# Cross attention of an eight-batch transformer step: k, q, x and masks prepared two batches ahead, rows of maxima sent from GpSimd, set-up woven into the first runs

## The chip, the cores and the metric

One core of a Trainium2 chip runs the whole program in one launch. The metric is the device time of that launch in microseconds; lower is better. A core has five engines with an instruction stream each (TensorE, VectorE, ScalarE, GpSimd, SyncE, in rows PE, DVE, ACT, POOL, SP) that work side by side and wait for each other by semaphores, and 16 DMA engines that move data for whoever issues a transfer.

## The reference

x is (8, 512, 256) in float32, with a context of the same shape. Four residual layers follow each other; in each, ln() is a layer norm without weights:

```python
x = x + feature_attention(ln(x), ctx, ctx)          # softmax over the sequence, per feature
x = x + experts(ln(x))                              # 8 experts, top 2
# the layer that the change touches: 16 heads of 16
q, k, v = heads(ln(x) @ Wq.T + bq), heads(ctx @ Wk.T + bk), heads(ctx @ Wv.T + bv)
scores = where(mask == 0, -1e9, q @ k.T / 4)
x = x + merge(softmax(scores) @ v) @ Wo.T + bo
x = x + gated_self_attention(ln(x))                 # 8 heads of 64, top 3 gates
```

The mask holds ones alone in these inputs. The program tests that at run time (a flag) and runs a loop without mask products when nothing is masked; the one thing that it then still takes from the mask is rv, which says for each query whether any key is left.

## The kernel before, in words

The layers are blocks of their own, one after the other; each block ends when all five engines have. The change lies in the block `cross_attention`. Before it, `combine` loads the weights and the context of batch 0. After it come `self_gates` and `self_attention`.

**Units and runs.** The 16 heads are four groups of 4. A unit is one group of one batch: 32 units, four for each batch, in a loop over batches (`pe.Fori(0, B)`, written once for each engine). A unit has 16 slots (4 heads by 4 blocks of 128 keys or queries) in 8 runs of two. In each slot TensorE makes two score products of 64x512: `score_b` (L915), the scores of this unit with keys on partitions, which ScalarE exponentiates (L1020), and `score_a` (L901), the scores of the unit two later with queries on partitions, of which VectorE takes the maximum of each row (L1108). The maxima must be known before the exponentials: they enter `score_b` as two extra rows of the stacked q. In even runs TensorE also multiplies the exponentials by the values (`values`, L921).

**Stacks.** q and k are split into a head and a rest part (float32 from two reduced parts). The parts of all heads go to DRAM (`store`, 1 MB for q, 1 MB for k) and come back group by group as stacks of 3 x 16 rows of each half, by `load_stack(g)`: 14 DMAs a group, issued by SP when the exponentials of unit g are done. `score_a` of group 0 of batch b+1 is in unit 2 of batch b, that of group 1 in unit 3, of groups 2 and 3 in units 0 and 1 of the next iteration.

**Jobs.** All other TensorE work shares one PSUM bank, `misc`, and so goes in a fixed order, one job a run at most, written out in `JOBS` as (name, unit, run), each after the score products and values of its run:
- m: transposes the maxima of the next unit (L837). ScalarE copies them, GpSimd splits them in two rows (`split_rows`), and SP sends them into the stack by four DMAs (`send_rows`).
- k0, k1, q0, q1, v0, v1: halves of the projections of the next batch; xT0, xT1: transposes of its normed x; rv: from the transposed mask. For q GpSimd makes the parts (`split_q`), for v it spreads the values (`move_values`).
- n0 to n3: transposes of a unit's output, divided by the sums on VectorE; t0, t1, o0, o1: the output projection of the batch before.

TensorE, in order, waits before a job until `misc` is free, and for v and k until the context is in (`ctx_in`). What an engine's stream has behind a waiting instruction waits too.

**Set-up.** `FIRST` lists the jobs for batch 0, which run one after the other. Then come the stacks, 16 runs of `score_a` alone (two units), the rows of maxima of unit 0, and the loop.

**SP's stream in an iteration**: masks of the next batch; rows for unit 1; store k (after k1); rows for unit 2; store q (after q1); stack 0, 1; rows for unit 3; stack 2; context of batch b+2; rows for the next unit 0; stack 3. Everything that SP issues goes in one queue.

Of the kernel before, what the change touches and what calls it, by code (L numbers as in the profile page):

```python
# [5 lines left out]
ALU = mybir.AluOpType  # L6
# [673 lines left out]
def cross_attention(nc, io, x, mv, rstd, ident, ones, bias, flag, q_parts, k_parts, weights, ctxT, w_in, ctx_in):  # L680
# [10 lines left out]
    with ExitStack() as ctx:  # L691
# [3 lines left out]
        ident16, tiny16 = m.sb("ident16", [P, P], BF16), m.sb("tiny16", [P, P], BF16)  # L695
        xn, xT = m.sb("xn", [P, TB, D]), m.sb("xT", [P, KC, S])
        nb, nbT = m.sb("nb", [P, 2, TB, S], BF16), m.sb("nbT", [P, 2, TB, S], BF16)
# [4 lines left out]
        k_stack = [m.sb(f"k_stack{g}", [P, HG // 2, S], F32R) for g in range(G)]  # L702
        negmax = m.sb("negmax", [P, 2, 2, 2, TB])
# [13 lines left out]
        nb_in, nbT_in = m.sem("nb_in"), m.sem("nbT_in")  # L717
# [19 lines left out]
        JOBS = [("m", 0, 0), ("k0", 0, 1), ("n0", 0, 2), ("k1", 0, 3), ("xT0", 0, 4), ("xT1", 0, 5), ("rv", 0, 6), ("q0", 0, 7),  # L737
# [3 lines left out]
        LAST = ["n0", "t0", "t1", "o0", "o1"]  # L741
        FIRST = ["k0", "k1", "xT0", "xT1", "rv", "q0", "q1", "v0", "v1", "m"]
# [10 lines left out]
        def nxt(b):  # L753
            return b + 1 if isinstance(b, int) else (b + 1) % B
# [1113 lines left out]
```

## Time and profile before

| | us |
|---|---|
| median of 3 runs | 2672.16 |
| lowest, highest | 2660.42, 2674.15 |
| the profiled execution | 2665.32 |
| its span, first to last instruction | 2663.6 |
| PE busy in the span | 2122.1 (80%) |
| DVE busy | 1484.3 (56%) |
| ACT busy | 926.3 (35%) |
| POOL busy | 836.8 (31%) |
| the cross loop, first score to last exponential | 1074.2 to 1677.5 |

The profile is one execution, with a start and a length for each instruction. Its views: busy time of each engine in chosen stretches, with the granted clock of TensorE (1 is 2.4 GHz, 0.5 is 1.2 GHz) and what the DMA engines moved; waits, put down to what ended them; instructions in order of time; and DMAs with the time from issue to landing. "L901" is line 901 of the kernel. A released wait stands in brackets behind the instruction that had waited.

### The profile page before, as it was taken

How to read it: one execution, taken by the hardware profiler on the slowest of the kernel's cores; microseconds unless marked ns; L12 is line 12 of the kernel's file. 1: busy time of each engine (PE TensorE's matmuls, PEld its weight loads, DVE VectorE, ACT ScalarE, POOL GpSimd, SP SyncE). 2: the span in 40 equal slices, each digit the busy share in tenths (PEclk: the TensorE clock that was granted, in tenths of full speed). 3: DMA queues.
4: the chain of work that ended last, by engine and by line, in shares of the span. 5: the costliest groups of instructions: out<-in, count | busy, mean ns of one | idle time of the engine just before them, and what ended most of it. 6: DMA issues, size and time to landing. Idle time of an engine off the chain costs nothing. (4 is left out here: it accounts for less than half of the span.)

```text
span 2663.6 us, 37640 instructions
## 1 busy us (share of the span) xinstructions
PE 2122.1 (80%) x11952; PEld 1389.3 (52%) x11961; DVE 1484.3 (56%) x2297; ACT 926.3 (35%) x1539; POOL 836.8 (31%) x753
## 2 busy tenths in 40 slices
PE   2340899999999505889888888838999999999997
PEld 1340899999999502333333333614545545554554
DVE  7820454545554344567666666544656656656655
ACT  2410333333333200455555555312333333333332
POOL 0067553435550362122212222011323323333232
PEclk9999999999999856899999999669999999999999
DMA  3162332333322332232232232324233223223322
GB/s 126 63 243 101 111 115 79 117 122 110 122 78 65 109 88 88 89 102 89 82 104 84 87 98 86 118 53 95 58 73 86 65 68 86 69 61 86 76 56 64
DMA packets 149071, 244.68 MB, mean 92 GB/s; under 512 B 22502, under 2 KB 71310, under 8 KB 146698
## 3 DMA queue, kind: packets, MB, share of 16 engines
q1 hardware_dynamic: 109762, 164.07, 21.9%
q0 software_dynamic: 11104, 44.06, 4.8%
q10 hardware_dynamic: 28160, 35.99, 4.2%
q8 instruction: 25, 0.41, 0.1%
q14 instruction: 20, 0.16, 0.0%
HBM read 120.48 MB, written 67.04 MB: 70 GB/s over the span
## 5 line engine op out<-in xcount | busy, mean ns | idle before, releaser
L1108 DVE TENSOR_REDUCE ca_negmax<-ca_na 128x2 f32<-128x1024 f32 x272 | 332.4, 1224 | 153.6 <-PE ca_na L901 153.6
L1020 ACT ACTIVATE ca_pr<-ca_st 128x512 f32<-128x512 f32 x512 | 278.9, 597 | 206.6 <-PE ca_st L915 205.6
L901 PE MATMUL ca_na<-ca_k_stack,ca_q_stack 64*128 64x512 f32 x544 | 222.7, 489 | 59.0 <-DMA ca_q_stack<-ca_zrow 55.6
L592 DVE TENSOR_TENSOR ex_h<-ex_up,ex_sg 128x512 f32<-128x512 f32 x136 | 94.1, 692 | 306.8 <-ACT ex_sg L555 197.4
L1706 DVE TENSOR_REDUCE sa_negmax<-sa_na 128x1 f32<-128x512 f32 x272 | 182.7, 674 | 130.8 <-PE sa_na L1527 126.5
L915 PE MATMUL ca_st<-ca_q_stack,ca_k_stack 64*128 64x512 f32 x512 | 210.6, 473 | 29.5 <-ACT ca_pr L1020 26.5
L515 PE MATMUL ex_gp<-ex_xp,moe_gu_p 128*128 128x256 f32 x1632 | 221.8, 286 | 1.4 <-DVE ex_xp L578 1.4
L515 PE MATMUL ex_up<-ex_xp,moe_gu_p 128*128 128x256 f32 x1632 | 218.4, 284 | 0.0
L528 PE MATMUL ex_yp<-moe_dn_p,ex_hp 128*128 128x256 f32 x1632 | 208.8, 286 | 11.3 <-DVE ex_hp L582 11.3
L515 PEld LDWEIGHTS ex_gp<-ex_xp,moe_gu_p 128*128 128x128 f32 x1632 | 206.1, 193 | 2.4 <-DVE ex_xp L578 1.8
L528 PEld LDWEIGHTS ex_yp<-moe_dn_p,ex_hp 128*128 128x128 f32 x1632 | 198.8, 192 | 15.2 <-DVE ex_hp L582 15.2
L515 PEld LDWEIGHTS ex_up<-ex_xp,moe_gu_p 128*128 128x128 f32 x1632 | 206.2, 193 | 0.0
L1694 POOL TENSOR_TENSOR sa_acc<-sa_acc,sa_pr 128x1024 f32<-128x1024 f32 x64 | 151.4, 2366 | 170.3 <-ACT sa_pr L1645 170.3
L1690 POOL TENSOR_TENSOR sa_acc<-sa_pr 128x1024 f32<-128x1024 f32 x32 | 75.1, 2348 | 386.5 <-ACT sa_pr L1645 386.5
L253 POOL TENSOR_TENSOR moe_gu_p<-moe_gu_raw,all_ones 128x512 fp32r<-128x512 f32 x64 | 85.9, 1377 | 287.0 <-PE ex_mark L532 263.8
L1645 ACT ACTIVATE sa_pr<-sa_st 128x1024 f32<-128x1024 f32 x128 | 131.1, 1024 | 107.5 <-PE sa_st L1536 107.5
L915 PEld LDWEIGHTS ca_st<-ca_q_stack,ca_k_stack 64*128 64x128 f32 x512 | 83.6, 191 | 152.3 <-ACT ca_pr L1020 98.7
L921 PE MATMUL ca_av<-ca_pr,ca_vw 128*32 128x512 f32 x1056 | 148.0, 635 | 0.0
L1535 PE MATMUL sa_st<-sa_q,sa_k 128*128 128x512 f32 x256 | 146.2, 571 | 0.0
L1543 PE MATMUL sa_av<-sa_pr,sa_vw 128*64 128x512 f32 x528 | 141.8, 617 | 0.0
L582 DVE TENSOR_TENSOR ex_hp<-ex_h,ex_hp 128x512 fp32r<-128x512 f32 x136 | 130.1, 960 | 2.0
L874 PE MATMUL ca_misc<-cross_ctxT,cross_wk 128*128 128x512 f32 x72 | 38.1, 655 | 113.3 <-DVE ca_zrow L1149 106.8
(261 smaller groups left out, 3798.1 us busy)
## 6 DMA issues: line engine op xcount, KB each, us to landing
sa_q<-sa_qh SPq DMA_DIRECT2D x140, 128.0 KB
sa_k<-sa_kh SPq DMA_DIRECT2D x140, 128.0 KB
ex_raw_m<-masks ACTq DMA_DIRECT2D x34, 512.0 KB, 3.8
moe_gu_raw<-gateupT POOLq DMA_DIRECT2D x8, 2048.0 KB, 8.2
ca_q_stack<-q_parts SPq DMA_DIRECT2D x216, 64.0 KB
ca_k_stack<-k_parts SPq DMA_DIRECT2D x216, 64.0 KB
expert_rows<-rt_zeros SPq DMA_DIRECT2D x20, 512.0 KB, 15.9
k_parts<-ca_kp SPq DMA_DIRECT2D x9, 1024.0 KB, 4.3
```

Source lines behind the costliest of these rows:

```text
L515: last = pe.matmul(out[:, f, :], gu_p[e % 2][:, wr, c, col:col + P], xp[:, xr, c, :], start=(n == 0), stop=(n == 3 * KC - 1))
L528: last = pe.matmul(yp[:, i, :], hp[:, hr, f, i * P:(i + 1) * P], dn_p[e % 2][:, wr, f, :], start=(n == 0), stop=(n == 3 * FC - 1))
L901: last = pe.matmul(na[r % 2][:, i, :], q_stack[g][rows, i, t * P:(t + 1) * P], k_stack[g][rows, i, :], start=not masked, stop=True)
L915: pe.matmul(st[i][:, :], k_stack[g][rows, i, t * P:(t + 1) * P], q_stack[g][rows, i, :], start=not masked, stop=True).then_inc(st_full, 1)
L921: last = pe.matmul(av[32 * h:32 * h + 32, :], vw[:, g, t, h, :], pr[:, t % 2, h % 2 * 2 + h // 2, :], start=(t == 0), stop=(t == TB - 1), ...
L1020: act.activation(pr[:, s // HG % 2, s % HG, :], st[s % 2][:, :], ACT.Exp, scale=DK ** -0.5).then_inc(exp_done, 1)
L1108: dve.tensor_reduce(negmax[:, g % 2, 1 - r % 2, :, r // 2], na[r % 2][:, :, :], AX.X, ALU.max, negate=True).then_inc(max_done, 1)
L1535: pe.matmul(out, k1[c][:, h, t * P:(t + 1) * P], q1[c][:, h, :], start=True, stop=False)
L1543: last = pe.matmul(av[h * H:(h + 1) * H, :], vw[:, c, t, h * H:(h + 1) * H], pr[:, t, h, :], start=(t == 0), stop=(t == TB - 1), skip_grou ...
L1645: act.activation(pr[:, t, :, :], st[t % 2][:, :, :], ACT.Exp, scale=H ** -0.5).then_inc(exp_done, 1)
L1694: pool.tensor_tensor(acc[:, :, :], acc[:, :, :], pr[:, t, :, :], ALU.add).then_inc(acc_done, 1)
L1706: dve.tensor_reduce(negmax[:, par, h, t:t + 1], na[s % 2][:, :], AX.X, ALU.max, negate=True).then_inc(max_done, 1)
```

## The change

- k, q, xT and rv are prepared for batch b+2 in iteration b, in place of b+1; v still for b+1. `JOBS` deals the same 21 jobs to other runs: the tail of the batch before (t, o) comes first, then v and rv, then k, then q.
- k reads a context buffer of its own, `ctxK`, loaded two batches ahead; v still reads `ctxT`. The transposed masks get a third buffer.
- SP's iteration: masks, transposed masks, context for v (b+1), context for k (b+2); the four stacks, each when its unit's exponentials are done; then a wait for all four, the store of k and the store of q. The first four stand at the head of the loop, where they follow the stores of the iteration before.
- The rows of maxima are sent by GpSimd, in `split_rows`, right behind the split; `send_rows` is gone from SP.
- Set-up: `FIRST` holds jobs for batch 0 and batch 1; those of batch 1 and the first m stand at places 2 to 13 among the 16 runs of `score_a` (None: before them, as till now). The two last iterations prepare batches that nobody uses.
- In ScalarE's stream the jobs of run 0 come ahead of the copy of the unit's output; VectorE norms x after run 0, not run 1; GpSimd spreads one group of values a unit and splits q in unit 3.

```diff
+        ctxK = m.sb("ctxK", [P, KC, S])
...
-        nb, nbT = m.sb("nb", [P, 2, TB, S], BF16), m.sb("nbT", [P, 2, TB, S], BF16)
+        nb, nbT = m.sb("nb", [P, 2, TB, S], BF16), m.sb("nbT", [P, 3, TB, S], BF16)
...
-        nb_in, nbT_in = m.sem("nb_in"), m.sem("nbT_in")
+        nb_in, nbT_in, ck_in = m.sem("nb_in"), m.sem("nbT_in"), m.sem("ck_in")
...
-        JOBS = [("m", 0, 0), ("k0", 0, 1), ("n0", 0, 2), ("k1", 0, 3), ("xT0", 0, 4), ("xT1", 0, 5), ("rv", 0, 6), ("q0", 0, 7),
-                ("m", 1, 0), ("q1", 1, 1), ("t0", 1, 2), ("t1", 1, 3), ("n1", 1, 4),
-                ("m", 2, 0), ("v0", 2, 1), ("n2", 2, 2), ("v1", 2, 5),
-                ("m", 3, 0), ("n3", 3, 2), ("o0", 3, 3), ("o1", 3, 7)]
+        JOBS = [("m", 0, 0), ("n0", 0, 3), ("xT0", 0, 4), ("t0", 0, 5), ("xT1", 0, 6), ("t1", 0, 7),
+                ("m", 1, 0), ("v0", 1, 1), ("n1", 1, 2), ("o0", 1, 3), ("v1", 1, 5), ("rv", 1, 7),
+                ("m", 2, 0), ("k0", 2, 1), ("n2", 2, 2), ("o1", 2, 3), ("k1", 2, 5),
+                ("m", 3, 0), ("q0", 3, 1), ("n3", 3, 3), ("q1", 3, 5)]
         LAST = ["n0", "t0", "t1", "o0", "o1"]
-        FIRST = ["k0", "k1", "xT0", "xT1", "rv", "q0", "q1", "v0", "v1", "m"]
+        FIRST = [("k0", 0, None), ("k1", 0, None), ("xT0", 0, None), ("xT1", 0, None), ("rv", 0, None), ("q0", 0, None), ("q1", 0, None),
+                 ("v0", 0, None), ("v1", 0, None), ("xT0", 1, 2), ("xT1", 1, 3), ("rv", 1, 5), ("k0", 1, 6), ("m", 0, 7),
+                 ("k1", 1, 9), ("q0", 1, 11), ("q1", 1, 13)]
...
+        def batch(name, b):
+            return b + 1 if name[0] == "v" else b + 2
...
-            def send_rows(g, a):
-                sp.wait_ge(ml_ready, a + 1)
-                for r in range(2):
-                    for j in range(2):
-                        row = j * HALF + RM + r
-                        sp.dma_start(q_stack[g][row:row + 1, :, :].bitcast(F32).rearrange("a i (t n) -> a (i t) n", n=P),
-                                     mrow[j * 2 * TB:(j + 1) * 2 * TB, r, :].bitcast(F32)).then_inc(m_in, 16)
+            load_context(sp, io, ctxK, ck_in, 1)
+            load_bias_T(0, 0)
+            load_bias_T(1, 1)
             load_bias(0, 0)
             sp.wait_ge(set_up, SETUP)
-            store(kp, k_parts, misc_free, k_stored, FIRST.index("k1") + 1)
+            store(kp, k_parts, misc_free, k_stored, first("k1", 0) + 1)
             store(qp, q_parts, qp_ready, q_stored, KC)
             sp.wait_ge(k_stored, 16)
             sp.wait_ge(q_stored, 16)
             for g in range(G):
                 load_stack(g)
-            sp.wait_ge(misc_full, FIRST.index("v1") + 1)
-            load_context(sp, io, ctxT, ctx_in, 1)
-            send_rows(0, 0)
+            for g in range(G):
+                sp.wait_ge(stack_in[g], LOAD)
+            store(kp, k_parts, misc_free, k_stored, first("k1", 1) + 1)
+            store(qp, q_parts, qp_ready, q_stored, 2 * KC)
             with sp.Fori(0, B) as b:
                 sp.wait_ge(exp_done, b * G * SLOTS + 2)
-                for g in range(G):
-                    sp.wait_ge(stack_in[g], b * LOAD + LOAD)
-                load_bias(nxt(b), (b + 1) % 2)
-                send_rows(1, b * G + 1)
-                store(kp, k_parts, misc_free, k_stored, b * nj + (nf + number("k1") + 1))
-                send_rows(2, b * G + 2)
-                store(qp, q_parts, qp_ready, q_stored, b * KC + 2 * KC)
+                load_bias((b + 1) % B, (b + 1) % 2)
+                load_bias_T((b + 2) % B, (b + 2) % 3)
+                load_context(sp, io, ctxT, ctx_in, (b + 1) % B)
+                load_context(sp, io, ctxK, ck_in, (b + 2) % B)
                 for g in range(G):
                     sp.wait_ge(exp_done, b * G * SLOTS + ((g + 1) * SLOTS + 2))
...
                    if g == 0:
                         sp.wait_ge(k_stored, b * 16 + 32)
                         sp.wait_ge(q_stored, b * 16 + 32)
                     load_stack(g)
-                    if g == 1:
-                        send_rows(3, b * G + 3)
-                    if g == 2:
-                        load_context(sp, io, ctxT, ctx_in, (b + 2) % B)
-                        send_rows(0, b * G + 4)
-            for g in range(G):
-                sp.wait_ge(stack_in[g], LOAD * (B + 1))
-            sp.wait_ge(ctx_in, 16 * (B + 2))
+                for g in range(G):
+                    sp.wait_ge(stack_in[g], b * LOAD + 2 * LOAD)
+                store(kp, k_parts, misc_free, k_stored, b * nj + (nf + number("k1") + 1))
+                store(qp, q_parts, qp_ready, q_stored, b * KC + 3 * KC)
+            sp.wait_ge(k_stored, 16 * (B + 2))
+            sp.wait_ge(q_stored, 16 * (B + 2))
+            sp.wait_ge(ctx_in, 16 * (B + 1))
+            sp.wait_ge(ck_in, 16 * (B + 1))
             sp.wait_ge(nb_in, 16 * (B + 1))
+            sp.wait_ge(nbT_in, 16 * (B + 2))
...
-                    pe.wait_ge(nbT_in, b * 16 + 16)
+                    pe.wait_ge(nbT_in, 32 if isinstance(b, int) else b * 16 + 16)
...
-                    pe.wait_ge(ctx_in, b * 16 + 16)
+                    now = isinstance(b, int) and b == 0
+                    if now:
+                        pe.wait_ge(ctx_in, 16)
+                    else:
+                        pe.wait_ge(ck_in, b * 16)
                     for i in range(KC):
-                        last = pe.matmul(misc[:, :], wk[:, i, c * P:(c + 1) * P], ctxT[:, i, :], start=(i == 0), stop=(i == KC - 1))
+                        last = pe.matmul(misc[:, :], wk[:, i, c * P:(c + 1) * P], (ctxT if now else ctxK)[:, i, :], start=(i == 0), stop=(i == KC - 1))
...
+                    pe.wait_ge(ctx_in, b * 16 + 16)
                     for t in range(2):
...
-                    for s in range(SLOTS):
-                        score_a(g, 0, s, g, masked)
-                    if g == 0:
-                        max_rows(nf - 1, 0, 0)
+                    for r in range(RUNS):
+                        for s in (2 * r, 2 * r + 1):
+                            score_a(g, 0, s, g, masked)
+                        for n, (name, b, spot) in enumerate(FIRST):
+                            if spot == g * RUNS + r:
+                                if name == "m":
+                                    max_rows(n, 0, 0)
+                                else:
+                                    prepare(n, name, b)
...
-                                    prepare(job, name, b + 1)
+                                    prepare(job, name, batch(name, b))
             pe.wait_ge(w_in, 16 * 8)
-            for n, name in enumerate(FIRST[:-1]):
-                if n == 0:
-                    pe.wait_ge(set_up, SETUP)
-                prepare(n, name, 0)
+            pe.wait_ge(set_up, SETUP)
+            for n, (name, b, spot) in enumerate(FIRST):
+                if spot is None:
+                    prepare(n, name, b)
...
+                        for n, name in jobs_at(g, r):
+                            if name[0] in "kxmt":
+                                evacuate(b * nj + (nf + n), name, batch(name, b))
                         if r == 0:
                             take(u, b * nj + nf + (number(f"n{g - 1}") + 1 if g else 0))
-                        for n, name in jobs_at(g, r):
-                            if name[0] in "kxmt":
-                                evacuate(b * nj + (nf + n), name, b + 1)
...
+                pool.wait_ge(ml_ready, a + 1)
+                pool.tensor_tensor(tick[:, :], ones[:, 0:1], ones[:, 0:1], ALU.mult)
+                for r in range(2):
+                    for j in range(2):
+                        row = j * HALF + RM + r
+                        pool.dma_start(q_stack[g][row:row + 1, :, :].bitcast(F32).rearrange("a i (t n) -> a (i t) n", n=P),
+                                       mrow[j * 2 * TB:(j + 1) * 2 * TB, r, :].bitcast(F32)).then_inc(m_in, 16)
...
+            split_rows(first("m", 0), 0, 0)
+            for c in range(KC):
+                split_q(c, first(f"q{c}", 1), 1)
             with pool.Fori(0, B) as b:
                 for g in range(G):
                     u = b * G + g
-                    split_rows(b * nj + (nf + [n for n, j in enumerate(JOBS) if j[0] == "m"][g]), u + 1)
+                    split_rows(b * nj + (nf + [n for n, j in enumerate(JOBS) if j[0] == "m"][g]), (g + 1) % G, u + 1)
                     if g == 0:
                         move_values(G - 1, u + G - 1, None)
                     if g == 1:
-                        split_q(1, b * nj + (nf + number("q1")), b + 1)
                         add_bias(b)
-                    if g == 0:
-                        split_q(0, b * nj + (nf + number("q0")), b + 1)
-                    for i in {2: (0, 1), 3: (2,)}.get(g, ()):
-                        move_values(i, u + (G - g + i), b * nj + (nf + number("v1")))
+                    if g:
+                        move_values(g - 1, u + G - 1, b * nj + (nf + number("v1")))
+                    if g == 3:
+                        for c in range(KC):
+                            split_q(c, b * nj + (nf + number(f"q{c}")), b + 2)
...
+            normalise(1, 1)
             for g in range(2):
                 for r in range(RUNS):
                     maximum(g, r, g)
+                    for n, (name, b, spot) in enumerate(FIRST):
+                        if spot == g * RUNS + r and name[0] not in "xm":
+                            evacuate(n, name, b, None, None)
             with dve.Fori(0, B) as b:
                 for g in range(G):
                     u = b * G + g
                     for r in range(RUNS):
                         maximum(g + 2, r, u + 2)
-                        if (g, r) == (0, 1):
-                            normalise(b + 1, (b + 1) % B)
+                        if (g, r) == (0, 0):
+                            normalise(b + 2, (b + 2) % B)
                         for n, name in jobs_at(g, r):
                             if name[0] not in "xmt":
-                                evacuate(b * nj + (nf + n), name, b + 1, u + 1, (b + (B - 1)) % B, b + 1)
+                                evacuate(b * nj + (nf + n), name, batch(name, b), u + 1, (b + (B - 1)) % B, b + 1)
```

## Rows read from the trace of the kernel before

**Rows 1.** Busy time by stretches: us, engines busy (instructions), TensorE clock, DMA share, GB/s.

```profile
1066.00:1071.00 5.00, 4.62 (x9) 1.99 (x8) 4.64 (x5) 0.00 (x0) 0.00 (x0) 0.50 0.37 97
...
1150.00:1225.00 75.00, 64.69 (x347) 26.77 (x344) 48.74 (x54) 41.48 (x79) 15.61 (x29) 0.93 0.30 93
...
1392.00:1394.00 2.00, 1.99 (x18) 0.95 (x16) 1.58 (x2) 2.00 (x6) 0.00 (x0) 1.00 1.03 384
...
1419.00:1425.00 6.00, 5.66 (x19) 2.30 (x20) 2.27 (x2) 2.41 (x5) 0.89 (x2) 0.50 0.44 123
```

**Rows 2.** Waits, 1150 to 1600: who waited, total us, times, longest.

```profile
PE ca_na L901 <- DMA ca_q_stack<-ca_zrow: 34.6, 6, 5.8
```

**Rows 3.** TensorE in order of time: start, us; starts of runs, and one end of waiting.

```profile
1398.24 0.49 PE L915 MATMUL ca_st<-ca_q_stack,ca_k_stack 64*128 64x512 f32 x1
...
1402.81 0.50 PE L915 MATMUL ca_st<-ca_q_stack,ca_k_stack 64*128 64x512 f32 x1
...
1406.39 0.50 PE L915 MATMUL ca_st<-ca_q_stack,ca_k_stack 64*128 64x512 f32 x1
...
1413.08 0.49 PE L915 MATMUL ca_st<-ca_q_stack,ca_k_stack 64*128 64x512 f32 x1 [0.45 <-ACT ca_pr L1020]
...
1419.34 0.79 PE L901 MATMUL ca_na<-ca_k_stack,ca_q_stack 64*128 64x512 f32 x1 [5.77 <-DMA ca_q_stack<-ca_zrow]
...
1437.11 0.49 PE L915 MATMUL ca_st<-ca_q_stack,ca_k_stack 64*128 64x512 f32 x1 [0.44 <-ACT ca_pr L1020]
...
1440.51 0.50 PE L915 MATMUL ca_st<-ca_q_stack,ca_k_stack 64*128 64x512 f32 x1 [0.54 <-ACT ca_pr L1020]
...
1445.80 0.50 PE L915 MATMUL ca_st<-ca_q_stack,ca_k_stack 64*128 64x512 f32 x1
...
1448.64 0.50 PE L915 MATMUL ca_st<-ca_q_stack,ca_k_stack 64*128 64x512 f32 x1 [0.45 <-ACT ca_pr L1020]
...
1453.15 0.49 PE L915 MATMUL ca_st<-ca_q_stack,ca_k_stack 64*128 64x512 f32 x1
```

**Rows 4.** SP's queue in order of time: start, us of the issue.

```profile
1377.08 0.33 SPq L773 DMA_DIRECT2D ca_q_stack<-q_parts  x1
...
1385.99 0.41 SPq L760 DMA_DIRECT2D ca_nb<-mask_bias  x1
...
1406.41 0.37 SPq L765 DMA_DIRECT2D q_parts<-ca_qp  x1
```

**Rows 5.** DMA issues: number, KB each, median us from issue to landing.

```profile
k_parts<-ca_kp SPq DMA_DIRECT2D x9, 1024.0 KB, 4.3
...
ca_nbT<-mask_bias SPq DMA_DIRECT2D x9, 512.0 KB, 4.9
...
cross_ctxT<-ctxT SPq DMA_DIRECT2D x10, 512.0 KB, 3.7
...
cb_got<-expert_outs,all_place POOLq DMA_INDIRECT x64, 2.7
```

**Rows 6.** ScalarE and GpSimd: a table load, a split, and the gathers, grouped.

```profile
1378.62 1.28 ACT L1020 ACT_TABLE_LOAD   x1 [1.57 <-PE ca_st L915]
...
1382.31 0.44 POOL L1051 TENSOR_TENSOR ca_mrow<-ca_mfull,ca_mrow 16x128 fp32r<-16x128 f32 x1
...
L645 POOL DMA_INDIRECT cb_got<-expert_outs,all_place x64 | 64.0, 1000 | 133.9 <-PEq L620 114.7 <-issue 19.2
```

**Rows 7.** In order of time: start and end of the set-up's scores, the loop, the block.

```profile
1007.89 3.75 PE L874 MATMUL ca_misc<-cross_ctxT,cross_wk 128*128 128x512 f32 x4 [106.78 <-DVE ca_zrow L1149]
...
1049.54 0.80 PE L901 MATMUL ca_na<-ca_k_stack,ca_q_stack 64*128 64x512 f32 x2 [8.00 <-DMA ca_q_stack<-ca_zrow]
...
1074.19 0.79 PE L915 MATMUL ca_st<-ca_q_stack,ca_k_stack 64*128 64x512 f32 x1 [3.01 <-DMA ca_q_stack<-ca_mrow]
...
1676.37 1.08 ACT L1020 ACTIVATE ca_pr<-ca_st 128x512 f32<-128x512 f32 x2 [0.75 <-PE ca_st L915]
...
1690.89 0.69 DVE L1142 TENSOR_TENSOR all_x<-ca_misc,all_x 128x512 f32<-128x512 f32 x1 [2.09 <-PE ca_misc L845]
```

More of the change, by code:

```diff
@@ L702, in cross_attention @@
         k_stack = [m.sb(f"k_stack{g}", [P, HG // 2, S], F32R) for g in range(G)]
+        tick = m.sb("tick", [P, 1])
         negmax = m.sb("negmax", [P, 2, 2, 2, TB])
@@ L751, in number, with first @@
             return next(n for n, j in enumerate(JOBS) if j[0] == name)
-        def nxt(b):
-            return b + 1 if isinstance(b, int) else (b + 1) % B
+        def first(name, b):
+            return next(n for n, j in enumerate(FIRST) if j[:2] == (name, b))
+        def batch(name, b):
+            return b + 1 if name[0] == "v" else b + 2
         @block.sync
@@ L867, in prepare @@
                 if name == "rv":
-                    pe.wait_ge(nbT_in, b * 16 + 16)
+                    pe.wait_ge(nbT_in, 32 if isinstance(b, int) else b * 16 + 16)
                     for t in range(TB):
-                        last = pe.matmul(misc[:, :], tiny16[:, :], nbT[:, b % 2, t, :], start=(t == 0), stop=(t == TB - 1))
+                        last = pe.matmul(misc[:, :], tiny16[:, :], nbT[:, b % 3, t, :], start=(t == 0), stop=(t == TB - 1))
                 elif name[0] == "k":
-                    pe.wait_ge(ctx_in, b * 16 + 16)
+                    now = isinstance(b, int) and b == 0
[3 more added lines that the diff above has]
+                        pe.wait_ge(ck_in, b * 16)
                     for i in range(KC):
-                        last = pe.matmul(misc[:, :], wk[:, i, c * P:(c + 1) * P], ctxT[:, i, :], start=(i == 0), stop=(i == KC - 1))
+                        last = pe.matmul(misc[:, :], wk[:, i, c * P:(c + 1) * P], (ctxT if now else ctxK)[:, i, :], start=(i == 0), stop=(i == KC - 1))
                 elif name[0] == "x":
@@ L913, in score_b @@
                 if masked:
-                    pe.matmul(st[i][:, :], ident16[:, :], nbT[:, b % 2, t, :], start=True, stop=False)
+                    pe.matmul(st[i][:, :], ident16[:, :], nbT[:, b % 3, t, :], start=True, stop=False)
                 pe.matmul(st[i][:, :], k_stack[g][rows, i, t * P:(t + 1) * P], q_stack[g][rows, i, :],
@@ L1008, in _ @@
             act.wait_ge(set_up, SETUP)
-            for n, name in enumerate(FIRST):
+            for n, (name, b, spot) in enumerate(FIRST):
                 if name[0] in "kxm":
-                    evacuate(n, name, 0)
+                    evacuate(n, name, b)
             with act.Fori(0, B) as b:
@@ L1075, in _ @@
             for c in range(KC):
-                split_q(c, FIRST.index(f"q{c}"), 0)
+                split_q(c, first(f"q{c}", 0), 0)
             for g in range(G - 1):
-                move_values(g, g, FIRST.index("v1"))
-            split_rows(nf - 1, 0)
+                move_values(g, g, first("v1", 0))
+            split_rows(first("m", 0), 0, 0)
+            for c in range(KC):
+                split_q(c, first(f"q{c}", 1), 1)
             with pool.Fori(0, B) as b:
@@ L1156, in _ @@
             normalise(0, 0)
-            for n, name in enumerate(FIRST[:-1]):
-                if name[0] != "x":
-                    evacuate(n, name, 0, None, None)
+            for n, (name, b, spot) in enumerate(FIRST):
+                if spot is None and name[0] != "x":
+                    evacuate(n, name, b, None, None)
+            normalise(1, 1)
             for g in range(2):
@@ L1162, in _ @@
                     maximum(g, r, g)
+                    for n, (name, b, spot) in enumerate(FIRST):
+                        if spot == g * RUNS + r and name[0] not in "xm":
+                            evacuate(n, name, b, None, None)
             with dve.Fori(0, B) as b:
```

3 lines of the change are left out of this document (2 added, 1 removed).

## The prediction

> **What bounds the kernel now.** I read first the busy table by stretches, then the waits of the loop, then the instructions in order of time. The loop of the cross attention runs from the first score at 1074.19 to the last exponentials, which end at 1676.37 + 1.08 = 1677.45 [rows 7]: 603.3 us for 8 batches, 75.4 a batch. In it TensorE is busy 64.7 of 75 us at a mean clock of 0.93, VectorE 48.7, ScalarE 41.5, GpSimd 15.6 [rows 1]. So TensorE's stream is the bound, with the waits in it. One stands out in the waits: 34.6 us in 6 times, 5.8 each, for the stacks of the next batch [rows 2]. At 1413.5 TensorE comes to the first row score of batch b+1 (start of the third unit) and goes on at 1419.34, after 5.77 us [rows 3]. The reason stands in SP's order: q of batch b+1 is stored at 1406.41 [rows 4], which lands 4.3 us later as k's does [rows 5]; only then are the 14 copies of stack 0 issued. After the wait TensorE runs at the lower level, 1.2 GHz (granted 0.50, 1419 to 1425) [rows 1]. The third unit takes 1437.11 - 1413.08 = 24.03 us. Priced by pairs of runs from quiet places (below) the same jobs make m+v 4.57, n 3.60, v1 4.51, empty 2.84: 15.5. So the stall costs 8.5 us: 5.8 of wait, 2.8 of slow clock. The period without it would be about 66.6.
>
> **Prices of the jobs.** One bank for all jobs, so what a job costs depends on its run. An even run carries 4 value products, an odd one none. From the starts of the score products [rows 3], each two runs apart unless said:
> - m in the even run, q in the odd: 1402.81 - 1398.24 = 4.57
> - two transposes: 1406.39 - 1402.81 = 3.58
> - n and nothing, nothing and nothing: 1413.08 - 1406.39 = 6.69 for four runs
> - m and nothing: 1440.51 - 1437.11 = 3.40
> - n and o: 1445.80 - 1440.51 = 5.29
> - nothing, after a heavy job: 1448.64 - 1445.80 = 2.84
> - nothing and o: 1453.15 - 1448.64 = 4.51
>
> **The new order of jobs, quiet.** The jobs of a batch are the same 21; they are dealt anew. Unit 0: m, (-,n0), (xT0,t0), (xT1,t1). The iteration's exponential table load of 1.28 us [rows 6] holds up the first run; I add 0.4. 3.40 + 0.4 + 3.2 + 3.58 + 3.7 = 14.3. Here 3.2 is estimated for a short job in an odd run, between the empty 2.84 and the two transposes' 3.58. Unit 1: m+v0 4.57, n1+o0 5.29, v1 4.5, rv 3.1: 17.5. Unit 2: m+k0 4.57, n2+o1 5.29, k1 4.5, empty 2.84: 17.2. Unit 3: m+q0 4.57, n3 3.2, q1 4.5, empty 2.84: 15.1. Sum 64.1, 2.5 under the 66.6, since k1 and q0 no longer stand in runs already full. Ends: 63.4 to 65.5.
>
> **The old stall goes.** k and q of batch b+1 are now stored a whole iteration before, so stack 0 is issued when its unit ends and has all of unit 1 (17.5 us) for an issue and landing that took 1377.08 to 1385.99, 8.9 us [rows 4]. Nothing there is late.
>
> **What is late next: the context for v0.** This is the step on which the sum hangs. The copy of the context that v reads moved from unit 3 to SP's loop head, and both stores moved ahead of that, to the tail of the iteration. Count from E, the end of unit 3's exponentials. SP issues stack 3 from E to E+7, and waits for all stacks: E+8.9, by the same 8.9 us. Then in one queue: k store (1 MB), q store (1 MB), then from about E+10.8 (about 1 us for the loop's branch) masks (0.5 MB), transposed masks (0.5 MB), the context of b+1 (0.5 MB), the context of b+2. A saturated stretch moves 384 GB/s with a DMA share of 1.03 [rows 1]. A k store alone lands after 4.3 us [rows 5], of which 1.05 MB at 384 GB/s is 2.7, so 1.6 us pass before the data moves. Up to and with the context of b+1 3.67 MB are queued: 9.6 us from E+10.5, hence E+20.1, and with 0.8 for the end of a load (an alone context takes 3.7: 1.6 + 1.4 + 0.7 [rows 5]) E+20.9. TensorE reaches v0 in run 1 of unit 1. Unit 0 starts 0.4 us before E (its first score waits only for the last but one exponential, 1.08 / 2 long [rows 7]); 14.3 for unit 0 and 2.8 to the place of the job make E+16.7. It waits 4.2 us. Nothing else can run: TensorE is in order, and unit 1's scores are behind v0. Ends: 0 if a later load passes the stores at the head of the queue, 5.8 (the old stall) if the six transfers drain at 300 GB/s.
> The two mask loads of the old kernel show the queue in small: the second lands 4.9 us after its issue, a load alone 3.7 [rows 5]. The Trainium skill (DMA: Bandwidth & Descriptors, section on queues, rings and completion order) says that each engine consumes descriptors in ring order; by that rule the order above is right. Its fit in the section on the anatomy of one DMA is 2.0 us plus bytes at 436 GB/s: an estimate by it puts the landing at E+19.3, the wait at 2.6 us and the total 11 us lower.
> The old wait of 5.8 us let the clock fall and cost 2.8 besides. I take 2.9 for this one: it strikes v0 itself, all TensorE work (3.75 us for such a job at the low level [rows 7] against half of it at 2.4 GHz), and the values behind it. Ends 1.5 to 3.9. Period 64.1 + 4.2 + 2.9 = 71.2, in 7 iterations. The first has no such wait: its q store is issued about 1.6 us after its start and the context lands near +10.
>
> **The rows of maxima on GpSimd.** Four DMAs a unit leave SP and stand on GpSimd, behind the split. The trace has no such small copy on this queue; nearest are the 64 gathers, 1.00 us each with 19.2 us over 63 gaps, 1.3 apiece [rows 6], landing in 2.7 [rows 5]. Unit 0: exponentials end 0.6 + 1.28 + 1.1 after its start (a first product, the table load, two exponentials), maxima copied by +3.3, two splits of 0.45 [rows 6] to +4.3, a tick, four issues to +9.7, landed +12.4; needed at +14.3. The other units are longer. Behind the issues wait move_values (1.3 us) and the q splits, which SP wants only at E+9. So 0, with 1.9 us in hand; 0 to 1 us an iteration by these rows. The Trainium skill (the same page, section Issuing engines are not separate DMA queues) speaks against counting on a queue of one's own, since all share 16 engines; it changes no term here, as I count no gain.
>
> **Set-up.** TensorE starts the scores at 1049.54 when stack 0 lands [rows 7], unchanged, as all before it is. The 16 runs took till about 1071.2, VectorE-paced (4.64 of 5 us), clock 0.50; then 3.01 us wait for the rows of maxima, which sat behind SP's issues [rows 1, 7]. That wait goes: -3. Seven jobs come in: xT0, xT1, rv, k0, k1, q0, q1. At 1.2 GHz TensorE has 4.62 of 5 us busy [rows 1], so jobs add nearly all they are: 0.9 twice, 1.5, 3.7 four times: 18. At 2.4 GHz half the products go and a run has 0.6 us free: 0.1 twice, 0.3, 1.4 four times: 6. With the jobs TensorE has hardly a gap, so I let the clock rise midway: 13. First score 10 later.
>
> **End.** VectorE's last addition ended at 1690.89 + 0.69 = 1691.58 [rows 7], E+14.1. Now SP, after the wasted stack 3, stores k and q of a batch nobody needs, and waits: 2.1 MB from E+10.5 at 384 GB/s, E+16.4. That is late now, by 2.3.
>
> **Sum.** First score 1074.2 - 3 + 13 = 1084.2; first iteration 64.5 (0.4 for what is left of the slow clock); 1084.2 + 64.5 + 7 x 71.2 = 1647.1; E 1647.5; end 1663.9 against 1691.6: -27.7. From the profiled execution's 2665.3 (1.7 over its span, which lies outside the change): 2637.6. The median of the three runs is 6.8 above that execution; I add half: 2641.
>
> **Rivals.**
> A, forecast: 0.64. Its own range 2622 to 2660.
> B, no wait at v0 (the context overtakes, or the queue drains sooner): period 64.1, 7 x 7.1 = 49.7 less, 2591. For it: only the one pair of mask loads shows queueing. Against: 3.67 MB must pass at 384 GB/s. 0.14.
> C, slower, rows of maxima late. If a small DMA holds GpSimd 2.7 us, rows land at +4.3 + 0.2 + 10.8 + 2.7 = +18.0: waits of 3.7, 0.5, 0.8, 2.9 at the four units, 7.9, and two falls of the clock, 5.7: 13.6 in place of 7.1 (v0's wait is swallowed). Over 7 iterations +45, in the first +13.6: 2700. It starts to cost at 1.8 us a DMA and beats the gain from about 2.4. Against: 1.3 in the gathers. 0.09.
> D, no change: the new wait is as long as the old (5.8, clock 2.9) and the redealt jobs save nothing (66.6): 75.3 in 7 iterations and 66.6 in the first, 594 against 603; set-up +10, end +2: +3, 2668 to 2671. Against: both are worked out from rows, and both would have to fail. 0.13.
> Range to 8 in 10: 2594 (half of B) to 2667. 0.5% is 13.4 us, about what a measurement of this kernel tells from none. Faster: B and nearly all of A, with a few of D: 0.76. Same 0.14, slower 0.10.
>
> **What would show it.** In the waits after: no wait of a row score for the stack; a wait of the v products for the context near 4.2 us, 7 times, ending near E+21, with clock 0.50 after it. Period 71.2; first score near 1084; stores of k and q landing before the context. DMA instructions on GpSimd near 1 us, and no score waiting for the rows. Wrong if v0 doesn't wait, if the clock holds through its wait (-20), or if the rows of maxima stop a unit.

## Result and profile after

| | before | after |
|---|---|---|
| median of 4 runs | 2673.0 us | 2631.8 us |
| ratio | | 0.9855, 95% interval 0.9828 to 0.9882 |
| profiled execution, its span | 2665.3, 2663.6 | 2634.6, 2632.8 |
| cross attention, first issue on SP to the next block's first | 693.7 | 653.3 |
| of it: start to first score | 75.8 | 78.4 |
| iteration 0 | 78.4 | 64.2 |
| iterations 1 to 7, each | 75.0 | 70.7 |
| last exponential to the next block | 14.7 | 16.1 |

The kernel is faster by 1.45%, with an interval from 1.2 to 1.7%, and the medians are 41 us apart; 2641 was forecast. Every execution of the kernel after is faster than every one of the kernel before. The four parts of the block add up to -40.4: +2.6, -14.3, -30.2, +1.5. The profiled executions are only 30.7 apart. Of the 10 us between, 2.7 lie ahead of the block and 7 behind it, in code that did not change (see the last section). Below, "period" is the mean distance from the last exponential of one iteration to the last of the next, over iterations 1 to 7: 75.1 before and 70.6 after.

The loop after, in the busy table by stretches (columns as in [rows 1]). 1150 to 1600 is the loop; the next two are the new wait and what comes behind it; 1366 to 1368 is the crowd of transfers; the last two are the set-up's runs.

```profile
1150.00:1600.00 450.00, 402.13 (x2179) 171.50 (x2183) 304.10 (x335) 261.05 (x500) 154.94 (x307) 0.95 0.40 111
...
1372.50:1377.50 5.00, 0.46 (x4) 0.02 (x2) 1.23 (x1) 1.56 (x4) 4.58 (x8) 0.80 1.06 375
1377.50:1383.00 5.50, 5.44 (x20) 3.18 (x20) 1.12 (x2) 0.90 (x2) 0.89 (x1) 0.56 1.12 170
...
1366.00:1368.00 2.00, 2.00 (x16) 0.80 (x15) 1.72 (x2) 2.00 (x5) 0.00 (x0) 1.00 1.01 370
...
1055.00:1060.00 5.00, 5.00 (x15) 2.77 (x14) 2.88 (x4) 1.17 (x2) 0.00 (x0) 0.50 0.42 118
1060.00:1066.00 6.00, 4.75 (x12) 1.70 (x12) 4.27 (x5) 0.69 (x1) 0.00 (x0) 0.87 0.35 106
```

The waits after, 1150 to 1600 (who waits, total us, times, longest). The stack's wait of [rows 2] is gone; this one stands in its place, before v0, the first v product of a batch:

```profile
PE ca_misc L895 <- DMA cross_ctxT<-ctxT: 32.1, 7, 4.7
```

TensorE in order of time, iteration 4 after: the starts of its units 0 to 3 and of the next unit 0, with v0 inside unit 1.

```profile
1355.41 0.49 PE L924 MATMUL ca_st<-ca_q_stack,ca_k_stack 64*128 64x512 f32 x1 [0.45 <-ACT ca_pr L1034]
...
1370.20 0.50 PE L924 MATMUL ca_st<-ca_q_stack,ca_k_stack 64*128 64x512 f32 x1
...
1377.56 3.78 PE L895 MATMUL ca_misc<-cross_wv,cross_ctxT 128*128 128x256 f32 x8 [4.61 <-DMA cross_ctxT<-ctxT]
...
1394.34 0.49 PE L924 MATMUL ca_st<-ca_q_stack,ca_k_stack 64*128 64x512 f32 x1
...
1411.26 0.49 PE L924 MATMUL ca_st<-ca_q_stack,ca_k_stack 64*128 64x512 f32 x1 [0.45 <-ACT ca_pr L1034]
...
1426.13 0.49 PE L924 MATMUL ca_st<-ca_q_stack,ca_k_stack 64*128 64x512 f32 x1 [0.45 <-ACT ca_pr L1034]
```

The units take 14.8, 24.1, 16.9 and 14.9 us. In iteration 0, which has no wait, they take 15.2, 17.2, 16.9 and 14.9. At 1377.56 v0 is the first thing that TensorE does after 4.61 us without work, and it runs at 1.2 GHz: 3.78 us, where v1 at 1389 takes 1.99. The granted clock reads 0.56 there, from 1.00 before the wait.

What v0 waits for stands in SP's queue (start, us of the issue) and in the DMA issues (number, KB each, median us from issue to landing):

```profile
1362.18 0.65 SPq L787 DMA_DIRECT2D ca_q_stack<-ca_zrow  x1
1365.09 0.38 SPq L776 DMA_DIRECT2D k_parts<-ca_kp  x1
1365.59 0.43 SPq L776 DMA_DIRECT2D q_parts<-ca_qp  x1
1366.91 0.41 SPq L769 DMA_DIRECT2D ca_nb<-mask_bias  x1
1367.71 1.01 SPq L772 DMA_DIRECT2D ca_nbT<-mask_bias  x1
1368.91 1.23 SPq L612 DMA_DIRECT2D cross_ctxT<-ctxT  x1
```

```profile
k_parts<-ca_kp SPq DMA_DIRECT2D x10, 1024.0 KB, 4.4
...
ca_nbT<-mask_bias SPq DMA_DIRECT2D x10, 512.0 KB, 8.5
cross_ctxT<-ctxT SPq DMA_DIRECT2D x9, 512.0 KB, 8.6
...
ca_q_stack<-ca_mrow POOLq DMA_DIRECT2D x132, 4.0 KB, 3.1
```

The last exponentials of the iteration before end at 1355.85 (E). The context is issued at E+13.1 and takes 8.6 us to land, where it took 3.7 in the old place [rows 5]. What was queued ahead of it moves without a break, but not at one rate (the last three columns are the clock, the DMA share and GB/s):

```profile
1366.00:1370.70 4.70, 4.68 (x32) 2.23 (x31) 3.40 (x3) 3.99 (x9) 0.00 (x0) 1.00 1.02 368
1370.70:1373.00 2.30, 2.26 (x16) 0.63 (x15) 1.42 (x2) 1.98 (x6) 0.25 (x1) 1.00 0.97 234
1373.00:1376.80 3.80, 0.00 (x0) 0.00 (x0) 1.23 (x1) 1.06 (x3) 3.63 (x8) 0.83 1.07 378
```

The 3.7 MB up to and with the context pass in these 10.8 us, 343 GB/s in the mean. Why the middle stretch moves less with the engines as busy stays open.

### The profile page after: what moved, and what is told of

It reads as the page before. It is cut to its first block and busy times, and to the rows that moved or that the text cites. A ratio compares the mean times of both kernels' runs of the same rounds, so it can differ in the third digit from the quotient of the medians.

```text
span 2632.8 us, 37781 instructions
## 1 busy us (share of the span) xinstructions
PE 2116.5 (80%) x11979; PEld 1393.4 (53%) x11989; DVE 1486.3 (56%) x2306; ACT 928.0 (35%) x1543; POOL 916.5 (35%) x922
## 5 line engine op out<-in xcount | busy, mean ns | idle before, releaser
L910 PE MATMUL ca_na<-ca_k_stack,ca_q_stack 64*128 64x512 f32 x544 | 209.0, 466 | 11.4 <-DMA ca_q_stack<-ca_zrow 9.3
L924 PE MATMUL ca_st<-ca_q_stack,ca_k_stack 64*128 64x512 f32 x512 | 202.3, 461 | 14.0 <-ACT ca_pr L1034 14.0
L1715 POOL TENSOR_TENSOR sa_acc<-sa_pr 128x1024 f32<-128x1024 f32 x32 | 75.1, 2348 | 386.4 <-ACT sa_pr L1670 386.4
L930 PE MATMUL ca_av<-ca_pr,ca_vw 128*32 128x512 f32 x1056 | 141.2, 608 | 0.9 <-ACT ca_pr L1034 0.9
L1746 DVE RECIPROCAL sa_rec<-sa_sumS 128x256 f32<-128x256 f32 x66 | 115.0, 1744 | 1.9 <-ACT sa_sumS L1640 1.9
```

Of the source, the lines that this page charges most:

```text
L910: last = pe.matmul(na[r % 2][:, i, :], q_stack[g][rows, i, t * P:(t + 1) * P], k_stack[g][rows, i, :], start=not masked, stop=True)
L924: pe.matmul(st[i][:, :], k_stack[g][rows, i, t * P:(t + 1) * P], q_stack[g][rows, i, :], start=not masked, stop=True).then_inc(st_full, 1)
L930: last = pe.matmul(av[32 * h:32 * h + 32, :], vw[:, g, t, h, :], pr[:, t % 2, h % 2 * 2 + h // 2, :], start=(t == 0), stop=(t == TB - 1), ...
```

## Experiments

"Block" is the cross attention as in the table. Each kernel differs from the one after unless said. Theory Q of the expectations is the prediction's: v0's wait comes from what SP has put ahead of the context, and it costs its own length and a fall of the clock. The kernel after, e1 and e8 were run four or five times; the other kernels once each, so for them the traces carry the argument and not a time alone.

**e1_ctx_unit2: the context of v loaded a batch ahead.**

```diff
@@ prologue
+            sp.wait_ge(misc_full, first("v1", 0) + 1)
+            load_context(sp, io, ctxT, ctx_in, 1)
@@ loop
-                load_context(sp, io, ctxT, ctx_in, (b + 1) % B)
...
                     load_stack(g)
+                    if g == 1:
+                        load_context(sp, io, ctxT, ctx_in, (b + 2) % B)
```

> The changed kernel with v's context loaded one unit after its last use (behind stack 1, for the batch after next) in place of the loop's head. Theory Q (the wait before v0 is the queue ahead of this copy, and the slow clock is that wait's): no wait before v0, TensorE's clock stays at 2.4 GHz in the loop, period 64.2 us in place of 70.6, 7 x 6.4 = 45 us less in all, 2587. Rival W (SP or the DMA engines are simply full in this stretch, another copy takes the wait over, for instance stack 0 or the rows of maxima for unit 1): the v products start on time, but a score waits, and the period stays above 68.

Measured: median 2583.5 us against 2668.1, ratio 0.9691 (0.9673 to 0.971). Block 607.8, period 64.2: five of the seven iterations take 63.8 and two take 65.1 (see the last section). No engine waits for the context between 1150 and 1600. The same stretch in the busy table:

```profile
1150.00:1600.00 450.00, 429.26 (x2387) 180.47 (x2393) 332.32 (x366) 284.94 (x545) 168.50 (x332) 0.99 0.43 116
```

TensorE is busy 429 of 450 us in place of 402, and the clock is 0.99 in place of 0.95. So the wait is worth 70.6 - 64.2 = 6.4 a batch in the mean, or 6.8 against the five quiet iterations: 4.6 of waiting and 1.8 to 2.2 of slow clock. The forecast was 64.2; rival W, that another copy takes the wait over, did not come. With e8 this is the best version of the study.

**e3_ctx_before_masks and e2_ctx_last: less and more ahead of it.** e3 moves the one line of the context ahead of both mask loads; e2 moves it behind the other context load.

> v's context load ahead of the two mask loads, behind the two stores: 1 MB less ahead of it. Theory Q: wait before v0 4.6 - 2.7 = 1.9 us; if the clock then holds, period 66.1, if it falls, 67.9. Rival F (sharing, whatever the order): wait 4.6. The run also tells what a short wait does to the clock.

> The two context loads at the loop's head change places: 0.5 MB more ahead of v's. Theory Q: 1.4 us more of wait before v0, 6.0 in place of 4.6, period 72. Rival F (the copies in flight share the engines whatever their order): the wait stays 4.6. Rival T (the time goes in SP's issue): 0.8 to 1.2 more, the length of one issue.

Measured: e3 2593.4 us, period 65.3; e2 2648.6 us, period 73.0. The waits of e3, then of e2, same stretch and columns as above:

```profile
PE ca_misc L895 <- DMA cross_ctxT<-ctxT: 8.9, 7, 1.6
```

```profile
PE ca_misc L895 <- DMA cross_ctxT<-ctxT: 41.3, 6, 7.2
```

1 MB less ahead takes 3.3 us off the mean wait (4.6 to 1.3; 2.7 was expected), 0.5 MB more adds 2.3 (1.4 was expected). So the wait grows with the bytes ahead, but not at one price. In e2 the context is the last of the six and lands at E+24.3, where the last of the six landed in the kernel after (1370.31 + 9.7, E+24.2). It moves beside the first copies of stack 0: from 1385.5 to 1389.2 the engines move 247 GB/s there at a share of 1.09. SP's issue is 1.2 us later too (rival T), but the engines have no gap from 1375 on, so the queue has work in the meantime; no run moved the issue alone. In e3 six of the seven waits are 1.3 to 1.6 us and one is 0.2. The period is 1.5 above the 63.8 of a quiet iteration: the short wait costs nothing beside its own length. v0 takes 2.0 us there, and the clock of 1150 to 1600 reads 1.00:

```profile
1150.00:1600.00 450.00, 424.24 (x2370) 177.72 (x2375) 331.48 (x364) 283.18 (x542) 168.50 (x336) 1.00 0.42 115
```

**e10_ctx_own_queue: the same load from ScalarE's queue.** Is it one queue's order, or the order over all?

```diff
@@ SP
-                load_context(sp, io, ctxT, ctx_in, (b + 1) % B)
@@ ScalarE
+                        if (g, r) == (0, 6):
+                            load_context(act, io, ctxT, ctx_in, (b + 1) % B)
```

> v's context load at the same place in time (about 12 us into the iteration) but issued by ScalarE, so in a queue of its own. Theory Q (order within one queue is what delays it): it shares the engines with SP's queue, some 2.8 us of data at half rate and 2.3 us of latency, so a wait of 0 to 2 us, period 64 to 66. Rival F (the engines take what was issued first whichever queue it came from): wait near 4.6 as now.

Measured: 2635.8 us, period 71.0, wait as before, 4.7 at most. ScalarE issues at 1373.80, E+13.3, about when SP did. The DMA queues of e10 in three stretches, 1374 to 1376, 1376 to 1378 and 1378 to 1380 (packets, MB, share of the engines; q1 is SP's, q10 ScalarE's):

```profile
q1 hardware_dynamic: 302, 0.62, 102.4%
...
q1 hardware_dynamic: 475, 0.56, 99.2%
...
q1 hardware_dynamic: 544, 0.54, 77.5%
q10 hardware_dynamic: 108, 0.22, 29.2%
```

The issues of the stretch 1374 to 1376 (which counts an issue still running) say how long the last two took to land:

```profile
ca_ctxK<-ctxT SPq DMA_DIRECT2D x1, 512.0 KB, 11.3
cross_ctxT<-ctxT ACTq DMA_DIRECT2D x1, 512.0 KB, 8.3
```

Up to 1378.5, 4.7 us after its issue, q10 moves no packet, though in iteration 0, with nothing else under way, the same load begins within 1.1 us of its issue; q1 has all 16 engines. Then the two share. So "in one queue" was too narrow a reason: another queue got nothing for 5 us and landed at E+21.6, no sooner than from SP's queue (E+21.7). But the order of issue doesn't hold over all queues either. SP issued the transposed masks 1.6 us and its context for k 0.4 us before ScalarE's load (1372.21, 1373.42, 1373.80). They took 10.0 and 11.3 us and so landed at 1382.2 and 1384.7, the load of ScalarE at 1382.1: once q10 moves, it passes what still stands in q1. Rival F, first issued first served, gave the wait right (4.6) and the order wrong. What holds q10 back for those 5 us stays open. The Trainium skill (DMA: Bandwidth & Descriptors, section Queues, rings and completion order) says that an engine alternates between the queues for which it has work, packet by packet; by that q10 should have moved from about 1375. The stretches to 1378 disagree, the one behind them agrees.

**e4_rows_sp and e12_ctx_unit2_rows_sp: the rows of maxima back on SP**, in the kernel after and in e1. What is GpSimd's queue worth?

```diff
@@ SP
+            send_rows(0, 0)
...
                 load_bias((b + 1) % B, (b + 1) % 2)
+                send_rows(1, b * G + 1)
...
                     load_stack(g)
+                    if g < 3:
+                        send_rows((g + 2) % G, b * G + (g + 2))
@@ GpSimd, split_rows
-                pool.wait_ge(ml_ready, a + 1)
-                pool.tensor_tensor(tick[:, :], ones[:, 0:1], ones[:, 0:1], ALU.mult)
-                ... (its four dma_start)
```

> The changed kernel with the rows of maxima on SP again (rows 1 behind the first mask load, rows 2, 3 and 0 behind stacks 0, 1 and 2), none on GpSimd. Theory Q: a queue of their own is worth what they would put ahead of v's context and behind the stores: four issues, 2.8 us later for the context, wait before v0 7.4 in place of 4.6; and the rows of unit 1 lie behind 2.5 MB, so that unit's first score waits 2 to 4 us of it. Period 73.4. Rival N (the queue of the rows is of no matter, as the old kernel's rows never stopped a unit in the loop): period 70.6.

> The context in unit 2, and the rows of maxima on SP again, as in e4_rows_sp. There v's wait and the rows' wait overlapped, so the queue of the rows seemed to be worth nothing. Theory H (it was hidden by v's wait): here unit 1's first score waits 4.7 us for its rows, which SP issues only behind both stores and a mask load, the clock falls, period 70 against e1's 63.8: the queue is then worth 6 us a batch. Rival N (it is worth nothing in any case): period 63.8.

Measured: e4 2635.9 us, period 70.6, block 653.6, the times of the kernel after. e12 2639.5 us, period 70.8, block 655.0, 47 more than e1. The waits of e4, then of e12:

```profile
PE ca_st L937 <- DMA ca_q_stack<-ca_mrow: 30.3, 7, 4.9
```

```profile
PE ca_st L940 <- DMA ca_q_stack<-ca_mrow: 30.6, 7, 4.9
```

In both the rows of unit 1 are late behind the stores, once a batch. In e4 no engine waits for the context: the wait for the rows swallows v0's, so moving the rows gained nothing in the kernel as it was changed. The 70.6 of e4 is rival N's number, but its rows do stop a unit; theory Q had added both waits. With v0's wait gone, the rows are what comes next: GpSimd's issuing is worth 6.7 us a batch in e1 (70.8 - 64.2). The moment of the issue explains it. In the kernel after GpSimd issues the rows of unit 1 at 1360.03, 5 us before the store of k; in e12 SP comes to them at E+10.9, after both stores. No run let SP send them ahead of the stores, so 6.7 is the worth against this place on SP and not against SP as such.

**e5_before_rows_pool and e5b_before_rows_pool_q_first: the move of the rows alone, in the kernel before.** e5 takes send_rows out of SP and lets split_rows issue them. e5b also calls `split_q(1, ...)` ahead of unit 1's split_rows.

> The kernel before, with only the rows of maxima moved to GpSimd's queue. In the old loop the rows never stopped a unit and stack 0 waited for the landing of q, which waits for GpSimd's split, not for SP. So: 3.0 us less in the set-up (the wait for the first rows), loop period 75.1 as before, cross block 690.7 against 693.7. Rival R (the 2.8 us of SP's time per unit are on the stack's path): period 72.3, 25 us less.

> As e5_before_rows_pool (the kernel before with the rows on GpSimd, whose period rose from 75.1 to 76), with one change: in unit 1 GpSimd splits q1 ahead of the rows of maxima. Theory P (the four issues, 2.1 us, stood ahead of the q split on GpSimd, and that split is on the path q store, stack 0, first score of the next batch): wait for stack 0 back to 5.0 to 5.8, period 74.4 to 75.1. Rival E (the rows' packets or their queue slow the stack's transfers): wait stays at 7.2, period 76.

Measured: e5 2679.3 us (the kernel before, run with it: 2674.3), period 76.1, block 696.5, start to first score 72.2 in place of 75.8. e5b 2673.9 us, period 74.9, block 688.6 in place of 693.7. The set-up gained as expected; that the loop would lose 1 us a batch was not. The waits of e5, then of e5b:

```profile
PE ca_na L887 <- DMA ca_q_stack<-ca_zrow: 43.0, 6, 7.2
```

```profile
PE ca_na L887 <- DMA ca_q_stack<-ca_zrow: 34.5, 6, 5.8
```

GpSimd of e5 in order of time shows why the old wait of 5.8 grew by 1.4:

```profile
1408.50 2.09 POOL L1043 DMA_DIRECT2D ca_q_stack<-ca_mrow  x4
1410.60 1.30 POOL L1025 TENSOR_TENSOR ca_qp<-ca_qf,all_ones 128x512 fp32r<-128x512 f32 x1
```

The four issues hold GpSimd for 2.1 us, and the split of q, on which the late stack hung, stands behind them. With the split put ahead of them (e5b) the wait is back at 5.8. In the kernel after, the last q split ends at 1356.14 and the store of q is issued at 1365.59, so there the q splits have 9 us to spare.

**e6_gap_filled, e7_setup_in_a_row, e8_both: the set-up's jobs placed otherwise.** TensorE waits 9.3 us for stack 0 before its first score. e6 puts xT0, xT1, rv and k0 of batch 1 ahead of the scores; e7 all seven jobs; e8 is e1 with xT0, xT1 and rv ahead and k0 at place 2. In all three VectorE norms x of batch 1 sooner, to feed the jobs; in e7 GpSimd also splits q ahead of the rows of maxima.

```diff
-                  ... ("xT0", 1, 2), ("xT1", 1, 3), ("rv", 1, 5), ("k0", 1, 6), ...
+                  ... ("xT0", 1, None), ("xT1", 1, None), ("rv", 1, None), ("k0", 1, None), ...
```

> The changed kernel with xT0, xT1, rv and k0 of batch 1 run before the scores, in the 9.3 us in which TensorE waits for stack 0, in place of places 2, 3, 5 and 6 among the runs. Expected: the wait for stack 0 nearly gone, the 16 runs shorter by the 4 us that these jobs add there; first score 4 us earlier, cross block 649 against 653. Rival: they add to the 16 runs less than I think (the clock had risen), 0 to 2 us.

> The changed kernel with all seven jobs of batch 1 before the first run, in a row. Each takes 1.3 to 3.8 us with its hand-over, in sum 19 to 24, of which 9.3 lie in the wait for stack 0: first score of the runs 10 to 14 us later, the 16 runs back to 21.7, so 4 to 8 us more in all. That is what weaving them in is worth. Rival: the clock stays high through the row and the 16 runs, and it costs nothing or gains.

> The version that the runs point to: v's context loaded in unit 2 (as in e1_ctx_unit2), and xT0, xT1 and rv of batch 1 run in the wait for stack 0, k0 at place 2; k0 is left among the runs because in e6_gap_filled it ran there at 1.2 GHz and held up the first score. Expected: the gain of e1 (cross block 607.9 us) and 2 to 3 us of set-up more, 605; time 2581, ratio to the kernel before 0.967. Rival: TensorE's clock falls in the 16 runs as in e6, and nothing is added to e1.

Measured, start to first score of the loop: after 78.4, e6 77.7, e8 78.1, e7 86.9. Whole: e6 2633.3, e7 2643.2; e8 2590.9, ratio 0.9688 (0.9674 to 0.9701), the same as e1. e6 and e8 gained 0.7 and 0.3 us there in place of the 2 to 4 expected; e7 lost 8.5, where 4 to 8 were. Filling the gap doesn't pay. In e6 and e7 the row of jobs outlasts the wait for the stack, and the 16 runs start 3.8 and 15.5 us later after the block's start. In e8 they start where they did, with three jobs fewer among them, and yet take 27.5 us against 27.9. The 16 runs from first to last in e1, in e8 and in e7 (no job but m among them):

```profile
1050.02:1077.93 27.91, 22.72 (x61) 10.06 (x62) 19.70 (x20) 2.80 (x5) 5.71 (x9) 0.76 0.45 131
...
1056.69:1084.18 27.49, 21.65 (x49) 8.55 (x50) 19.00 (x19) 1.63 (x3) 5.72 (x9) 0.69 0.45 122
...
1071.73:1092.64 20.91, 16.24 (x34) 7.02 (x34) 17.68 (x15) 0.26 (x1) 3.18 (x7) 0.55 0.71 232
```

The mean clock is 0.76 with seven jobs among the runs, 0.69 with four and 0.55 with none; in e6, with three, it is 0.71. The jobs among the runs keep TensorE in work and lift it towards 2.4 GHz; without them the runs alone, paced by VectorE, stay at or fall back to the lower level, as before [rows 1]. Only these traces say so; no run held the clock and moved the jobs.

## Why the prediction was right

- **The bound and the old stall.** Right. Every step that took time off the loop did so on TensorE's stream, and no score in the loop of the kernel after waits for a stack. The price of the old stall's slow clock, 2.8, rests on 3.60 for n, which no row shows; the rows give 6.69 - 2.84 = 3.85, and so 2.5.
- **The quiet period.** Forecast 64.1 (14.3, 17.5, 17.2, 15.1); iteration 0 took 64.2 (15.2, 17.2, 16.9, 14.9), a quiet iteration of e1 63.8. Sums of pairs of runs from quiet places carried over to a new deal of the same jobs. Unit 0 was 0.9 too low, the others 0.2 or 0.3 too high: that the sum fits to 0.1 is in part that they cancel.
- **The new wait at v0.** Place, number and cause were right: 7 times, 4.6 each against 4.2. TensorE came at E+17.1 (forecast E+16.7), the context landed at E+21.7 (E+20.9). The step let data move from E+10.5 (a store issued at E+8.9, and 1.6 us) at 384 GB/s, 9.6 us. The store was issued at E+9.2, data moved about 1 us behind it, from E+10.2, and took 10.8 us at 343 GB/s. The bound at 5.8 us of wait was said to be 300 GB/s; by the step's own sum 300 gives 6.9. SP issued the context only at E+13.1, but the engines had work all the while. The estimate by the fit of the Trainium skill (DMA: Bandwidth & Descriptors, section on the anatomy of one DMA; landing E+19.3) was 2.4 short: the measurement decides. The page gives that fit for DMAs issued by GpSimd; these are SP's. The reason "in one queue" was wrong in its scope (e10), without harm here, since all six were in SP's queue.
- **The clock's share.** 2.2 against 2.9 (1.8 against the mean of e1), inside 1.5 to 3.9. v0 itself is 1.8 of it, 3.78 against 1.99; what follows is back at 2.4 GHz by v1. Period 70.6 against 71.2.
- **The rows of maxima.** Cost 0, right, for an easier reason. The four issues took 2.1 us, 0.53 each, not 5.2; the gathers were a poor price for a plain copy of 4 KB, and rival C, that the rows come late, was further off than its 0.09. The step did not say what the move was worth in the loop: nothing here (e4), 6.7 a batch once v0's wait is gone (e12), against rows that SP sends behind the stores.
- **Set-up.** The one term that was off: +2.6 and not +10, 7.4 of the 12.7 us by which the block beat its forecast. The wait for the rows went (-3.0) and the scores began 0.7 sooner after the block's start. The seven jobs cost 27.9 - 21.7 = 6.2 (1051.62 to the first score at 1079.54, against 1049.54 to 1071.2), the low end of 6 to 18. The clock did rise midway: 0.50 at first, 0.87 in 1060 to 1066, where the second batch's k0 took 1.98 us, 0.76 over the whole. So the prices were too high. "Jobs add nearly all they are" was read from a stretch in which TensorE is busy 4.62 of 5 us [rows 1]; over all 16 runs of the kernel before it is idle for 4.8 us, room that the jobs could use in part (row below). Of the rest of the 12.7, 4.5 are the loop and 0.8 the end.

```profile
1049.54:1071.20 21.66, 16.84 (x33) 7.07 (x33) 17.62 (x15) 0.25 (x1) 0.90 (x2) 0.50 0.41 112
```

- **End.** +1.5 against +2.3. SP's wasted k and q stores are issued at 1646.85 and 1647.35, and the next block begins at 1654.43, E+16.1. VectorE's last addition ends 4.6 us earlier:

```profile
1649.13 0.69 DVE L1163 TENSOR_TENSOR all_x<-ca_misc,all_x 128x512 f32<-128x512 f32 x1 [2.09 <-PE ca_misc L849]
```

- **The total.** 2641 against 2631.8. That it is only 9 off is in part luck. The block beat its forecast by 12.7, but code outside the change ran 9.7 slower in the profiled execution (2.7 ahead, 7 behind): 3.0 there. The other 6 are medians: 3.4 were added to the forecast, and the median after lies 2.8 below its profiled execution. The kernel before itself spreads from 2660 to 2674.

## What to carry to other kernels

When a load is moved in a queue, count the bytes that are outstanding when it is issued, over all queues, and compare its landing with the moment at which the consumer comes; the change could have bought 11 us a batch and gave 6 to 7 back, because one load that had been early was put behind 3 MB of others. The cure was a load a batch ahead, in a quiet stretch; another queue did not help. A short wait and a long one are priced differently: one of 1.3 to 1.6 us cost its own length, one of 4.6 us cost 6.4 to 6.8. And when idle time is to take up new work, read it over the whole stretch and not from its busiest 5 us.

## What the runs showed of the hardware

- The clock may settle otherwise in code that did not change. The last four projections of the program in the kernel before, then in the kernel after (TensorE in order of time):

```profile
2646.39 3.75 PE L1515 MATMUL sa_misc<-self_wo,sa_outT 128*128 128x256 f32 x8 [5.12 <-POOL sa_outT L1683]
2650.87 1.99 PE L1515 MATMUL sa_misc<-self_wo,sa_outT 128*128 128x256 f32 x8
...
2656.82 2.00 PE L1515 MATMUL sa_misc<-self_wo,sa_outT 128*128 128x256 f32 x8
```

```profile
2608.60 3.75 PE L1540 MATMUL sa_misc<-self_wo,sa_outT 128*128 128x256 f32 x8 [5.12 <-POOL sa_outT L1708]
2613.43 3.78 PE L1540 MATMUL sa_misc<-self_wo,sa_outT 128*128 128x256 f32 x8
...
2624.00 3.78 PE L1540 MATMUL sa_misc<-self_wo,sa_outT 128*128 128x256 f32 x8
```

Both follow the same wait of 5.12 us. In one the clock is back at 2.4 GHz for the second projection, in the other it stays at 1.2 to the end, 7 us in all. Of the 13 traces seven are back by the second projection, five by the third, and only the kernel after not at all. The wait ahead is 4.82 us in six of the seven (5.12 in the kernel before) and 4.85 to 5.12 in the others. What decides between them stays open; 7 us are some 0.3% of the program, so a difference of that size between two single executions says nothing of a change.

- The same in small: two of e1's seven iterations are 1.4 us longer, and two of e8's, in e1 with the clock at 0.67 for 5 us of a stretch in which TensorE is never idle:

```profile
1275.00:1280.00 5.00, 5.00 (x28) 1.67 (x20) 3.38 (x5) 2.30 (x5) 2.49 (x7) 0.67 0.26 71
```

- SP's issue grows when much is outstanding: 0.4 us for the stores, 1.0 and 1.2 for the second mask and the context behind them. That put the issue of the context off by about 1 us; that it put off the landing is not shown, since the engines had work without a break.
- A load on a queue of its own moved no packet for 5 us while SP's queue filled the engines, and then shared them (e10).
